# New keys' value product in three fp32r passes, with loads and stores moved between two queues

## The reference

```python
q = rope(rmsnorm(x @ Wq.T))            # 32 query heads of 128
k = rope(rmsnorm(x @ Wk.T))            # 8 key heads
v = x @ Wv.T
kc = k_cache[block_table]              # 16 pages of 32 positions: 512 cached keys
vc = v_cache[block_table]
k_all = concat([kc, k]); v_all = concat([vc, v])      # 544 = 512 cached + 32 new
scores = einsum(q, k_all) * SCALE      # cached positions beyond the length are masked
o = einsum(softmax(scores), v_all)
return o @ Wo.T
```

## Time and profile before

| | |
|---|---|
| median of 3 runs | 1255.03 us |
| lowest, highest | 1254.48, 1257.87 us |
| profiled execution, its time | 1256.73 us |
| its span | 1254.8 us |
| attention stages | about 160 to 476 us and 785 to 1100 us |
| PE busy | 1228.1 us, 98% of the span |

### The profile page before, as it was taken

The page is one execution under the profiler, slowest core; times in us unless marked ns, Lnnn a source line. Parts: engine busy times, 40 slices in busy tenths (PEclk is TensorE's granted clock), DMA queues, the critical chain, the costliest instruction groups (busy, mean ns, idle before and its releaser), DMA issues.

```text
span 1254.8 us, 28770 instructions
## 1 busy us (share of the span) xinstructions
PE 1228.1 (98%) x7378; PEld 1031.9 (82%) x7378; DVE 808.2 (64%) x1736; ACT 788.1 (63%) x2259; POOL 749.5 (60%) x884
## 2 busy tenths in 40 slices
PE   7999999999999999999999999999999999999998
PEld 6788888899999997865777888888999999888756
DVE  6976666667666778951459667666766676655422
ACT  5666677778777774432346666777777777744320
POOL 4343467888888875433233443788888888844320
PEclk9999999999999999999999999999999999999999
DMA  6524288998999955306135252998899999534300
GB/s 206 194 92 149 95 232 220 230 232 233 236 236 237 229 159 177 142 8 194 68 105 184 84 172 91 243 220 227 224 234 240 231 238 239 121 116 153 89 30 34
DMA packets 147978, 214.82 MB, mean 171 GB/s; under 512 B 24949, under 2 KB 119479, under 8 KB 142136
## 3 DMA queue, kind: packets, MB, share of 16 engines
q1 hardware_dynamic: 134792, 206.96, 60.2%
q10 hardware_dynamic: 13104, 6.94, 1.9%
HBM read 203.33 MB, written 10.49 MB: 170 GB/s over the span
## 4 chain that ended last, share of the span: by engine, by line
PE 74%; SPq 15%; issue 5%; DVE 3%; ACT 1%; DMA 1%; ACTq 0%; DVEq 0%
PE PS L1139 12%; PE PS L1107 6%; SPq L485 6%; SPq L470 6%; PE PS L1206 5%; PE PS L1197 5%; PE PS L1001 5%; PE PS L1203 5%; PE PS L1005 5%; PE PS L999 5%; PE PS L1149 3%; PE PS L1248 2%; PE PS L985 2%; PE PS L1072 2%; PE PS L1237 1%
## 5 line engine op out<-in xcount | busy, mean ns | idle before, releaser
L630 POOL TENSOR_TENSOR kv_parts<-kv,k_hi 128x544 fp32r<-128x544 f32 x192 | 258.4, 1346 | 59.9 <-ACT k_hi L815 59.7
L1139 PE MATMUL PS<-probT,kv 128*128 128x128 f32 x2048 | 270.3, 275 | 0.0
L590 POOL TENSOR_TENSOR ring_parts<-ring,kv_parts 128x512 fp32r<-128x512 f32 x96 | 126.0, 1318 | 209.9 <-ACT kv_parts L693 181.6
L1139 PEld LDWEIGHTS PS<-probT,kv 128*128 128x128 f32 x2048 | 248.8, 192 | 0.0
L856 ACT ACTIVATE ring<-ring,smin 128x544 f32<-128x544 f32 x192 | 142.9, 744 | 86.9 <-DVE smin L1636 86.6
L1642 DVE COPY probT<-PS 128x512 f32<-128x512 f32 x256 | 175.5, 686 | 5.4 <-PE PS L1107 5.4
L1636 DVE CUSTOM_DVE_ANT_0 ring<-PS,mask,rq 128x544 f32<-128x544 f32 x192 | 149.7, 780 | 38.2 <-PE PS L1095 28.7
L652 POOL TENSOR_TENSOR ring_parts<-ring,kv_parts 128x512 fp32r<-128x512 f32 x64 | 85.0, 1332 | 95.1 <-ACT kv_parts L906 95.1
L815 ACT ACTIVATE k_hi<-kv 128x544 fp32r<-128x544 f32 x192 | 124.6, 650 | 15.5 <-DMA kv<-k_new 9.6
L618 POOL TENSOR_SCALAR ring<-ring,rinv 128x512 f32<-128x512 f32 x192 | 133.1, 693 | 0.0
L1676 DVE TENSOR_TENSOR qo_parts<-qo,kv_parts 128x512 fp32r<-128x512 f32 x64 | 85.3, 1339 | 54.1 <-ACT kv_parts L914 51.5
(11 more groups left out here) (218 smaller groups left out, 2743.9 us busy)
## 6 DMA issues: line engine op xcount, KB each, us to landing
kv<-in_kpages SPq DMA_DIRECT2D x512, 128.0 KB, 2.5
kv<-in_vpages SPq DMA_DIRECT2D x512, 128.0 KB
ring<-in_w SPq DMA_DIRECT2D x44, 1024.0 KB, 5.0
k_new<-kv ACTq DMA_DIRECT2D x16, 256.0 KB, 2.3
kv<-k_new SPq DMA_DIRECT2D x32, 128.0 KB, 2.5
kv<-v_new SPq DMA_DIRECT2D x32, 128.0 KB
kv<-in_xT SPq DMA_DIRECT2D x8, 256.0 KB, 5.2
ring<-in_w SPq DMA_DIRECT2D x8, 256.0 KB, 5.4
```

Source lines behind the costliest of these rows:

```text
L630: nc.gpsimd.tensor_tensor(kbuf_lo(par)[:, :, g, :], kbuf(par)[:, :, g, :], k_hi[:, e % 2, :].rearrange("p (j t) -> p j t", t=PSIZE), ALU.s ...
L1139: mm = nc.tensor.matmul(PS[:, at:at + D], vbuf(bpar)[:, c, gg * D:(gg + 1) * D], probT[:, g % 2, c * P:(c + 1) * P], start=(c == 0 and a = ...
```

## The change

Five things are changed.

1. `values_new` becomes three fp32r passes: `vnew_hi`·`spread_hi`, `vnew_lo`·`spread_hi`, `vnew_hi`·`spread_lo`.
2. The parts for it are made by three engines. ACT rounds the new values once a batch at the end of step 5 (`upper_values`, 128x256) and writes `spread_hi` in place of `spread`. POOL makes `vnew_lo` in step 7 (`lower_values`, 128x256). DVE makes `spread_lo` by four subtractions of 32x128 (`lower_spread`) at the end of steps 3 and 7. For the first batch of a half `upper_values` waits for `first_vnew_in`.
3. POOL lowers the first key of a group one step earlier, in steps 3 and 7, ahead of that step's scaling, and none in steps 0 and 4.
4. DVE takes the reciprocal of step `g-1`, not `g`, between the masking and the copy of step `g`.
5. SP issues the writes of the second V half (`store_values(1, m)`), three between its value pages of batch 0 and the fourth behind the new keys of batch 1. From batch 2 on ACT issues the load of the new keys (end of step 1) and of the new values (end of step 6), one batch ahead.

```diff
@@ SP @@
                     load_key_pages(par, pages, 0, NPP)
-                    load_new_keys(b, par)
                     sp.wait_ge(v_free, h * (HB - 1) + b - 1)
-                    load_new_values(b, par, v_in[par])
...
                     load_value_page(0, j, pages[j])
+                    if j % 4 == 3 and j < NPP - 1:
+                        store_values(1, j // 4, j // 4)
+                        sp.sem_inc(sp_past, 1)
...
                 load_new_keys(1, 1)
+                store_values(1, 3, 3)
                 for n in range(2):
                     sp.wait_ge(vn_out[n], 8 * KU * (h + 1))
                 load_new_values(0, 0, first_vnew_in)
@@ POOL @@
+                def lower_values(b, par):
+                    pool.wait_ge(vhi_ready, h * HB + b + 1)
+                    pool.sem_inc(pool_past, 1)
+                    nc.gpsimd.tensor_tensor(vnew_lo(par), vnew(par), vnew_hi(par), ALU.subtract).then_inc(vlo_ready, 1)
...
                     for g in range(HK):
-                        if g % GU < NS:
...
+                        if g % GU == NS and g < HK - 1:
+                            lower_key(b, par, g + 1)
+                        elif g == HK - 1 and not last:
+                            lower_key(b + 1, 1 - par, 0)
+                        elif 0 < g % GU < NS:
+                            lower_key(b, par, g)
                         if g >= 2:
                             scale_probs(b, g - 2, first)
                         elif not first:
                             scale_probs(b - 1, g - 2 + HK)
+                        if g == HK - 1:
+                            lower_values(b, par)
@@ ACT @@
-                    act.wait_ge(v_read, h * (2 * TILES) + TILES + m + 1)
-                    act.dma_start(vn_d[ds(h * HB + 4 * m, 4), :, D:2 * D]
...
+                def upper_values(b, par):
+                    if isinstance(b, int) and b == 0:
+                        act.wait_ge(first_vnew_in, 16 * (h + 1))
...
+                    nc.scalar.activation(vnew_hi(par), vnew(par), ACT.Copy).then_inc(vhi_ready, 1)
...
+                    if g == 5:
+                        upper_values(b, par)
+                    if g == 1 and not (first or last):
+                        load_new_keys(b + 1, 1 - par)
+                    if g == 6 and not (first or last):
+                        load_new_values(b + 1, 1 - par)
@@ PE @@
-                    nc.tensor.matmul(bank(6 + u), vnew(par)[:, u * D:(u + 1) * D], spread, start=False, stop=True)\
-                        .then_inc(o_done, 1)
+                    nc.tensor.matmul(bank(6 + u), hi, spread_hi, start=False, stop=False)
+                    nc.tensor.matmul(bank(6 + u), lo, spread_hi, start=False, stop=False)
+                    pe.wait_ge(spread_low, GU * (h * QUADS + b * UNITS + u + 1))
+                    nc.tensor.matmul(bank(6 + u), hi, spread_lo, start=False, stop=True).then_inc(o_done, 1)
@@ DVE @@
+                    if g <= HK and not (first and g == 0):
+                        k = (g - 1) % HK
+                        dve.wait_ge(exp_done, s)
+                        V.reciprocal(rinv[:, k:k + 1], rsum[:, k:k + 1]).then_inc(rinv_ready, 1)
...
+                    if g < HK and g % GU == 3 and not (first and g < GU):
+                        lower_spread(b if g > GU else b - 1, int(g < GU))
```

More of the change, by code:

```diff
@@ L453, in _, with store_values @@
             with sp.Fori(0, HALVES) as h:
[L454 to L457, removed]
+                def store_values(col, m, order):
+                    sp.wait_ge(v_read, h * (2 * TILES) + col * TILES + order + 1)
+                    sp.dma_start(vn_d[ds(h * HB + 4 * m, 4), :, col * D:(col + 1) * D]
+                                 .rearrange("b (t a) d -> (b t) a d", a=GU),
+                                 v_stage(col, m).rearrange("p (a d) -> p a d", a=GU)).then_inc(vn_out[m % 2], 16)
+                for order, m in enumerate((2, 3, 0, 1)):
+                    store_values(0, m, order)
                 with sp.Fori(0, 2) as i:
@@ L1621, in _, with lower_spread @@
                 norm_rows()
+                def lower_spread(b, u):
+                    dve.wait_ge(spread_ready, GU * (h * QUADS + b * UNITS + u + 1))
+                    if isinstance(b, int) and b == 0 and u == 0:
+                        dve.wait_ge(spread_clear, 2 * h + 2)
+                    dve.sem_inc(dve_past, 1)
+                    for a in range(GU):
+                        rows = slice(a * SEQ, (a + 1) * SEQ)
+                        V.tensor_tensor(spread_lo[rows, a * P:(a + 1) * P], PS[rows, 2560:2688],
+                                        spread_hi[rows, a * P:(a + 1) * P], ALU.subtract).then_inc(spread_low, 1)
                 def step(b, par, g, first):
@@ L1642, in step @@
                         V.tensor_copy(probT[:, (g - 3) % 2, :], bank(4)).then_inc(pt_main, 1)
-                    if first and g == 1:
-                        dve.wait_ge(exp_done, s)
-                        V.reciprocal(rinv[:, 0:1], rsum[:, 0:1]).then_inc(rinv_ready, 1)
-                    if g < HK and not (first and g == 0):
-                        dve.wait_ge(exp_done, s + 1)
-                        V.reciprocal(rinv[:, g:g + 1], rsum[:, g:g + 1]).then_inc(rinv_ready, 1)
-                        if g % GU == 1:
-                            nb, u = (b, 1) if g == 1 else ((b + 1) % HB, 0)
-                            dve.wait_ge(qhi_ready, h * (QUADS + 1) + b * UNITS + g // GU + 2)
-                            dve.sem_inc(dve_past, 1)
-                            lower_q(u, ds(nb * (HQ * SEQ) + u * GU * D, NS * D))
+                    if g < HK and g % GU == 1:
+                        nb, u = (b, 1) if g == 1 else ((b + 1) % HB, 0)
+                        dve.wait_ge(qhi_ready, h * (QUADS + 1) + b * UNITS + g // GU + 2)
+                        dve.sem_inc(dve_past, 1)
+                        lower_q(u, ds(nb * (HQ * SEQ) + u * GU * D, NS * D))
+                    if g < HK and g % GU == 3 and not (first and g < GU):
+                        lower_spread(b if g > GU else b - 1, int(g < GU))
                 for g in range(HK):
@@ L1670, in _ @@
                 step(HB - 1, 1, HK + 2, False)
+                lower_spread(HB - 1, 1)
                 def lower(head):
```

69 lines of the change are left out of this document (48 added, 21 removed).

## The result

The changed kernel takes 1267.48 us (median of 4, 1264.57 to 1268.04), the kernel before in the same session 1256.14 us (1254.48 to 1257.87): a ratio of 1.0079 [1.0067, 1.0092], slower by 0.8%. The forecast was 1256 us, no measurable change, with a range of 1246 to 1262; the measured time lies above all of it. The profiled execution took 1267.61 us, its span is 1265.8 us: 11.0 us more than the span before.

What follows compares the result with a forecast made beforehand. PE at its own pace bounds the kernel now, POOL's run after the change. Batches -2.8, half starts +5.6, SP -2.8, last products about 0.5: +0.5 on the profiled 1256.73, less 1.7, plus half a us: 1256 us, range 1246 to 1262.

Steps and rivals of the forecast that it cites:

- PE's product: Values product on PE: three fp32r passes instead of fp32 save 0.15 us each, 0.30 us a batch.
- POOL's run: Chain through POOL to PE's low part of head 2: 19.01 us a batch, gaining 0.10 us each, 2.8 in all.
- the head start of head 0: POOL's earlier lowering of a group's first key: no help to POOL's run, since it needs ACT's `k_hi`.
- SP's relief: SP's queue loses two loads per batch, so ACT's 9.6 us of waits end: net -2.8 us.
- The start of each half: Batch 0 of each half: new values land at 178.5, ACT waits, PE is 2.8 us late; +5.6 us together.
- The start costs nothing: Rival: batch 0's new values land before ACT asks, 5.6 us not lost; 1250.5 us, or 1245 with PE's pace; chance 0.07.
- PE's pace: Rival: PE still sets the batch time, 18.81 us, and 5.6 us more are won; 1250 us; chance 0.25.
- DVE blocks POOL: Rival: DVE's `lower_spread` subtraction holds POOL beside scaling 6; 1278 us, or 1267 with one stop; chance 0.08.

Runs made afterwards that it cites:

- e5: The changed kernel with POOL's `lower_values` moved from the end of step 7 to the end of step 6: 1262.19 us, 1.0041 of the kernel before.
- e10: The changed kernel with POOL's old order, the first key of a group lowered in its own step: 1271.37 us, 1.0107 of the kernel before.
- e2: The kernel before, with only the loads of new keys and new values from batch 2 on moved from SP to ACT: 1254.84 us, 0.9974.
- e12: The kernel before, with only the stores of the values' second column moved to SP: 1267.06 us, 1.0071.
- e9: The changed kernel with the stores of the values' second column given back to ACT: 1254.48 us, 0.9982 of the kernel before.
- e11: The changed kernel with ACT storing the second column again and `lower_values` at the end of step 6: 1249.41 us, 0.9940 of the kernel before.
- e4: The changed kernel with 18 added identity products on PE ahead of batch 1's first scores: 1265.46 us, 1.0057 of the kernel before.
- e3: The changed kernel with SP's last store ahead of batch 1's later key pages, and first new values loaded before batch 1's new keys: 1261.85 us, 1.0033.
- e13: e11 with only half of each value page loaded in the loop over batches 2 to 15: 1243.28 us, 0.9884 of the kernel before.

## Why the prediction was wrong

**PE's product.** Forecast -0.15 us a product, and right. Read in the forecast's own way, the stretch from L1200 to the second matmul of the next scores takes 324.07 - 322.35 = 1.72 us with the product and 326.39 - 325.36 = 1.03 without it, so the three passes cost 0.69 us against 0.85 before. Where POOL doesn't hold PE, as in e5, a batch takes 2 x 9.385 = 18.77 us, against the 18.81 that I gave for PE's own pace.

**POOL's run.** Right: 19.01 forecast, 19.09 to 19.10 measured, with the gap-free POOL and PE at L1151 behind it. The 19.11 that I set it against was one batch of two: before, the batches alternate between about 19.09 and 19.23, so the gain is 0.07 us a batch, not 0.10. And I held that the head start of head 0 "doesn't help this run". Its own use was hidden in my sum: with the old order (e10) the group is 0.23 us longer. And the statement that decided, the place of `lower_values`, I took as given; e5 shows 0.3 us a batch in it.

**SP's relief.** Right in sign and size: the waits for new keys are gone, e2 gives 0.26%, 3.3 us (net -2.8 forecast). It came with waits for key pages instead, 2.2 us after `in_kpages` once in the changed kernel.

**The start of each half.** This is the step that failed: "PE is 2.8 us late", +5.6 in all. The place and the mechanism, ACT standing in order at the first new values, were right; the term that was mis-sized is the time at which the first new values come, 178.5 by the forecast and 181.4 measured. Held against the old times as the forecast did, ACT's `k_hi` is 6.1 us late (181.76 against 175.66) and PE's step 3 of batch 1 6.3 (192.67 against 186.39); the second half adds 9.25 - 1.07 = 8.2. Together 14.5 us and not 5.6, and this is 8.9 of the 10.5 us between the forecast's change of the span and the measured one. (The 7.87 of the table is more than the 6.3 since batch 0 itself came 1.6 us earlier, so that ACT asked earlier and waited longer.)

Two terms made the values late. First, the landings: I took 2.7 and 2.5 us, both medians. Here SP went on 3.55 us after the store's issue (4.4 in the second half), and ACT 4.5 us after the load's (5.3): from the store to ACT's copy are 8.0 and 9.7 us, not 5.2 and a wake. While the store landed the DMA engines had a share of 0.53 (173.4 to 176.9), so other transfers may have held it. For the load it isn't a crowd of transfers ahead of it, since the share is 0.05 and 0.21 over 176 to 180; what part of it the value pages make, which follow the load by 1.7 us and fill the engines from 180 on (1.04), was not tried. Second, the store itself: I put it at 171.76 and added 1 us for the three stores ahead; it was issued at 173.42.

Two more things were at nothing or too small in the sum. I counted PE's idle time and not the clock that follows it: at 0.50 it costs 0.5 and 0.2 us net, so this is a small term. And I followed one victim of SP's stop, though 16 value pages stand in the queue behind it; I put what SP issues late at "about 1 us a half". e12, whose ACT doesn't ask for the new values, shows that SP's four stores are enough for a loss of 0.7%, with PE waiting for value pages and new values.

**The rivals.** "The start costs nothing" is what e9 makes nearly true, at 1254.5, and with PE's pace at 1249.4 (e11); the forecast had 1250.5 and 1245. "DVE blocks POOL" ended near the measured 1267 but is false: POOL's short scaling beside L1696 keeps its 0.28 to 0.31 us (321.97, 0.30 long, while L1696 runs from 321.59 for 1.23). The Trainium skill (SBUF — State Buffer, "Who interferes with whom") says that a DVE instruction with at most one input in SBUF, outside the modes that use two ports, doesn't contend with GpSimd. Here the trace agrees, and the time came from elsewhere. A time that fits is no proof of its mechanism.

## What to carry to other kernels

When an instruction that waits for a transfer's landing is put on a queue, price everything that queue issues behind it, not only the engine that asks first; here one store of 0.6 us on SP made value pages, new values or new keys late, whichever stood next. Bound a store that a load waits for by more than the sum of two medians (here 8.0 and 9.7 us against 5.2). When PE stands idle for some us, look for a slow clock behind it, and count of it only what no other engine's run covers (here 0.2 to 0.5 of 2 us). And a cheaper product pays only when nothing else holds the engine: here its gain came through when one POOL instruction was moved into a gap of its own (e5, 0.38%; 18.77 us a batch instead of 19.09).

## What the runs showed that was not expected

- PE's granted clock fell to 0.50 (1.2 of 2.4 GHz) while it stood idle for 4.73 us, and stayed there until 5 us after its restart. Shorter stops had the same effect: behind two of 1.39 and 1.00 us (e4, first half) the clock was 0.50 over 187 to 188, and behind two of 1.18 and 0.99 us (e3, first half) 0.50 over 182 to 184.
- A 256 KB store and a 128 KB load of the same data, one after the other, took 8.0 and 9.7 us from the store's issue to the use, while the DMA engines were nearly idle for 4 us of it (shares of 0.05 and 0.21).
- At a DMA share of 0.92 to 0.96 over 235 to 260 us, key pages come late by up to 1.4 us four times (e11); at 0.61 to 0.63 never (e13).
